# Exact attention scores on TensorE: one 128-row matmul for four heads, or one 25-row matmul for each head in four row groups

## The chip, the cores and the metric

The kernel runs on one core of one Trainium2 chip. The metric is the device time of one execution in microseconds (us); shorter is better. The figures shown are the median of several executions and, for the profile, one execution taken by the hardware profiler.

## The reference

64 sequences of 128 tokens with 128 features go through a gated block. Cut to what matters:

```python
def xattn(x, y):                                   # y: 120 context tokens of 96 features
    q, k, v = split_heads(x @ Wq + bq), split_heads(y @ Wk + bk), split_heads(y @ Wv + bv)   # 16 heads of 8
    scores = einsum('bhqd,bhkd->bhqk', q, k) / sqrt(8)
    return einsum('bhqk,bhkd->bhqd', softmax(scores), v) @ Wo + bo

def ffn(x):
    h = rms(x, n1_w)
    q, k, v = rms(heads(h @ wq.T), qn_w), rms(heads(h @ wk.T), kn_w), heads(h @ wv.T)
    scores = where(causal, einsum('bhqd,bhkd->bhqk', q, k) * 8 ** -0.5, -inf)
    ao = (softmax(scores) @ v) @ wo.T              # first 32 features set to 0
    x = x + ao
    xf = rms(x, n2_w)
    w = top-2 gates of softmax(xf @ gate_w.T)
    return x + w0 * o0(xf) + w1 * o1(xf) + w2 * o2(xf) + w3 * o3(xf)   # first 32 features of the sum set to 0

x = x + tanh(g_xattn) * xattn(layernorm(x), ctx)
x = x + tanh(g_ffn) * ffn(layernorm(x))
```

## The kernel before, in words

The 64 sequences are worked on in 16 groups of four (512 tokens). A group passes through five parts: N (layer norm, projections of the cross-attention), A (cross-attention), B (layer norm, projections of the self-attention), D (self-attention, gates, first expert layers) and M (the other expert layers, output). In one step all five parts run, each on another group, so the kernel is a pipeline: four written-out steps fill it (`RAMP`: `first_group` with N, `second_group` with N and A, `third_group` with N, A and B, `fourth_group` with all but M), a hardware loop runs 12 full steps (t = 3 to 14, order `SCHEDULE`, L160), and four written-out steps empty it (`TAIL`: `last_queries`, `last_self_keys`, `last_self_values`, `last_experts`).

The order of a step is a list written by hand. An entry (part, work, index, ring) is one use of a PSUM bank or a piece of work without one, and every engine walks the same list and does its share of each entry, in the list's order: TensorE fills the bank, ScalarE or VectorE drains it, and two semaphores for each bank, `filled` and `drained`, count the uses. The rings give the banks in turn: `w` has four, `s2` and `f` share the two banks s2a and s2b, `pv` and `t` have one each. `exact(part, b, first)` stands for two uses of the ring `s2`, `estimate` for four score tiles of a sequence, `values` for the four value matmuls of a sequence.

Attention is done in two passes. The *estimate* (work `s1`) computes scores in bfloat16, four row groups of TensorE at a time (L1299; for B with a causal term before it, L1295), and VectorE takes the negative maximum of each row (L1085). The *exact* scores (work `s2`, L1319 to L1336) are computed with float32r operands. For exactness a value is split in a high and a low part, and three products (high x high, low x high, high x low) are summed by stacking them along the contraction: 8 features x 3 = 24 rows a head. A 25th row adds the maximum of the estimate (the query operand holds it, the key operand holds ones).

Before, a chunk c of four heads is one matmul. The key operand `kst` has the four heads' rows interleaved (rows j, j + 4, ... below 96 belong to head j of the chunk, row 96 is ones), and the query operand `qd` has four copies of each column set, one for each head, with zeros in the rows of the other heads:

```python
qd = {p: sb("qd" + p, [P, HT, NT, TOK], F32R) for p in "AB"}
o = bank[0:k, :].rearrange("p (h q) -> p h q", h=HT)
mm(o, kst[p][:, c, b * k:(b + 1) * k], qd[p][:, :, c, b * P:(b + 1) * P],
   start=True, stop=True).then_inc(done, 1)
```

The matmul waits for its own bank only (L1333). ScalarE takes the exponential of the tile of 512 columns into one of eight slots of `probs` (L945). For D, GpSimd then zeroes what the causal mask hides, two tiles at a time (L812). The value matmuls (`pv`, L1337 to L1357) go in four column groups, one for each head j, and wait for the tile (b, c) alone.

The operands travel through DRAM. ScalarE and VectorE write the high and the low part of the projections (L855, L979); SyncE stores them to a scratch tensor (`store_split`, L581 to L590) and loads them back into the stacked rows (`load_stacks`, L592 to L602). The maxima are transposed on TensorE (`mT`, and for the first groups the halves `mH` and `mL`), copied by ScalarE, and brought by a DMA to the 25th row of the query operand: by SyncE (L664, L669), or by ScalarE's own queue for those that `maxima_by_act` (L559) names (L924). The zeros of the query operand are written once at the start, by VectorE (L1016, L1192), GpSimd (L705, L798) and ScalarE (`clear_queries`, L836 to L839). The ones of the key operand are written at L830 and L755.

GpSimd also makes the two causal factors of B's estimate (`causal_factor`, L710): that of the queries in the first step, that of the keys in the third, ahead of squaring B's projections (L823).

Of the kernel before, what the change touches and what calls it, by code (L numbers as in the profile page):

```python
# [31 lines left out]
P = 128  # L32
# [4 lines left out]
HD = 8  # L37
# [138 lines left out]
def second_group():  # L176

    return (one("N", "xT", 0, "pv") + one("N", "k", 0, "t") + one("N", "q", 0, "pv") + one("A", "mL")
            + exact("A", 0, 0) + exact("A", 0, 2) + estimate("A", 0) + exact("A", 1, 0) + exact("A", 1, 2) + values("A", 0)
            + estimate("A", 1) + exact("A", 2, 0) + exact("A", 2, 2) + one("A", "mH", 0, "t") + values("A", 1)  # L180
            + exact("A", 3, 0) + one("A", "oT", 0, "t") + exact("A", 3, 2) + estimate("A", 2) + values("A", 2)
            + one("A", "nT", 0, "t") + one("A", "wo", 0, "t") + values("A", 3) + one("N", "v", 0, "f") + estimate("A", 3)
            + one("A", "oT", 1, "f") + one("A", "nT", 1, "t") + one("A", "wo", 1, "t")
            + one("A", "base", 0, None) + one("A", "stats", 0, None) + one("N", "ctx", 0, None) + one("N", "load", 0, None)
            + one("A", "norm", 0, None))


def third_group():
# [4 lines left out]
            + exact("A", 2, 0) + exact("A", 2, 2) + one("B", "sums", 0, None) + one("N", "stats", 0, None) + one("B", "init", 0, None)  # L193
            + one("B", "root", 0, None) + values("A", 1) + exact("A", 3, 0) + exact("A", 3, 2) + one("B", "scale", 0, None)
            + one("A", "oT", 0, "t") + one("N", "norm", 0, None) + one("B", "qT") + one("B", "kT") + values("A", 2)
            + one("A", "nT", 0, "t") + one("A", "wo", 0, "t") + values("A", 3) + one("B", "v")
            + estimate("B", 0, "ffww") + one("N", "xT", 0, "t") + estimate("B", 1, "wwtp") + one("A", "oT", 1, "f")
            + estimate("B", 2, "fwww") + one("A", "nT", 1, "t") + one("B", "mH", 0, "t") + estimate("B", 3, "ffwp")
            + one("A", "wo", 1, "t") + one("A", "stats", 0, None) + one("N", "q") + one("A", "norm", 0, None)
            + one("N", "k") + one("N", "v"))  # L200


def fourth_group():

    order = of_parts("NABD")
    at = order.index(("D", "s2", (2, 0), "s2"))
    return order[:at] + one("D", "mL", 0, "t") + order[at:]


def last_queries():  # L210
# [4 lines left out]
    at = order.index(("D", "fill", ("e2_l1", 1), "f"))  # L215
# [1235 lines left out]
```

## Time and profile before

| | us |
|---|---|
| median of three executions | 1086.48 |
| lowest and highest | 1086.42 and 1088.23 |
| the profiled execution | 1085.92 |
| its span, first to last instruction | 1084.2 |

The span is the part of the profiled execution that the rows tell of; some 1.7 us lie around it. PE is TensorE's matmuls and PEld its weight loads. A float32 matmul shows as two records in the profile, one for each pass, and so does its load. The end of a matmul in the records is modelled, so the distance from one start to the next says more than the duration.

### The profile page before, as it was taken

The numbers are of one execution on the slowest core, as the hardware profiler recorded it, in microseconds if no ns is written. First come the engines' busy times: TensorE is split into PE (matmuls) and PEld (weight loads), VectorE is DVE, ScalarE is ACT, GpSimd is POOL, SyncE is SP. The second block draws the span as 40 slices with busy tenths as digits, with TensorE's granted clock in tenths as the row PEclk, the third lists the DMA queues.
The fourth block names the chain that finished last, engine by engine and source line by source line (L and its number), as shares of the span: only waits on it lengthen the run. The fifth ranks groups of instructions, "written<-read, shape, count | busy, mean of one in ns | idle before, by whom it ended". The sixth has DMA issues, their size and how long they took to land.

```text
span 1084.2 us, 26207 instructions
## 1 busy us (share of the span) xinstructions
PE 1011.1 (93%) x8649; PEld 628.9 (58%) x8649; DVE 790.0 (73%) x2172; ACT 736.9 (68%) x1334; POOL 338.4 (31%) x463
## 2 busy tenths in 40 slices
PE   7666799999999999999999999999999999999898
PEld 5343456666565566655665665566556565555465
DVE  8546787778778777877777777878777877784633
ACT  6464576677776768777676777767676777757353
POOL 5253315151330505133150514214141422404140
PEclk9779799999999999999999999999999999999999
DMA  6305233334322243333224343332233333221200
GB/s 231 121 27 195 86 101 103 127 115 143 110 94 94 90 126 124 133 114 111 93 73 124 130 127 114 123 99 84 97 129 127 114 134 104 84 67 62 68 1 19
DMA packets 77316, 114.26 MB, mean 105 GB/s; under 512 B 7776, under 2 KB 40160, under 8 KB 77152
## 3 DMA queue, kind: packets, MB, share of 16 engines
q1 hardware_dynamic: 76736, 111.51, 31.7%
q10 hardware_dynamic: 544, 2.28, 0.6%
q8 instruction: 22, 0.36, 0.1%
q14 instruction: 14, 0.11, 0.0%
HBM read 58.97 MB, written 53.74 MB: 104 GB/s over the span
## 4 chain that ended last, share of the span: by engine, by line
PE 64%; DVE 16%; ACT 13%; issue 6%; DMA 1%; ACTq 0%; POOL 0%; DVEq 0%
PE ps_pv L1356 9%; PE ps_w L1382 9%; PE ps_s2a L1335 7%; PE ps_s2b L1335 5%; PE ps_s2a L1394 5%; PE ps_s2b L1401 4%; ACT probs L945 4%; PE ps_t L1218 4%; DVE mpadB L1085 3%; PE ps_w L1401 3%; DVE mpadA L1085 3%; PE ps_w L1267 3%; PE ps_t L1369 3%; PE ps_w L1299 2%; PE ps_w L1218 2%
## 5 line engine op out<-in xcount | busy, mean ns | idle before, releaser
L945 ACT ACTIVATE probs<-ps_s2a 120x512 f32<-120x512 f32 (+1 forms) x256 | 153.6, 600 | 73.7 <-PE ps_s2a L1335 65.3
L1085 DVE TENSOR_REDUCE mpadB<-ps_w 128x4 f32<-128x512 f32 x240 | 148.8, 684 | 24.9 <-PE ps_w L1299 24.9
L1085 DVE TENSOR_REDUCE mpadA<-ps_w 128x4 f32<-128x480 f32 x224 | 131.5, 651 | 41.0 <-PE ps_w L1299 41.0
L945 ACT ACTIVATE probs<-ps_s2b 120x512 f32<-120x512 f32 (+1 forms) x256 | 153.5, 600 | 0.0
L812 POOL TENSOR_SCALAR_AFFINE_SELECT probs<-probs 128x1024 f32<-128x1024 f32 x128 | 140.2, 1095 | 0.0
L1382 PE MATMUL ps_w<-W,hid 128*128 128x96 f32 x1008 | 125.3, 278 | 1.8 <-DVE split_k L979 0.9
L1382 PEld LDWEIGHTS ps_w<-W,hid 128*128 128x128 f32 x1008 | 117.5, 192 | 12.0 <-issue 6.4
L776 POOL TENSOR_TENSOR rB<-vrB,neg_half 128x4 f32<-128x4 f32 x16 | 16.1, 1009 | 204.3 <-DVE veB L972 204.3
L1335 PE MATMUL ps_s2a<-qdA,kstA 128*120 128x512 f32 x128 | 68.5, 535 | 10.6 <-ACT probs L945 9.2
L1114 DVE SCALAR_TENSOR_TENSOR ym<-ps_w,gates,ym 128x96 f32<-128x96 f32 x192 | 47.6, 311 | 39.5 <-PE ps_w L1382 39.5
L1335 PE MATMUL ps_s2a<-qdB,kstB 128*128 128x512 f32 x128 | 65.2, 509 | 11.1 <-DMA qdB<-mTlB 4.5
L1394 PE MATMUL ps_s2a<-hid,W 128*128 128x512 f32 x152 | 74.5, 605 | 0.0
L949 ACT ACTIVATE oT<-ps_pv 128x512 f32<-128x512 f32 x64 | 38.3, 598 | 53.0 <-PE ps_pv L1356 53.0
L941 ACT ACTIVATE hid<-ps_s2a 128x512 f32<-128x512 f32 x75 | 45.0, 600 | 42.6 <-PE ps_s2a L1394 31.0
L1356 PE MATMUL ps_pv<-probs,VA 120*18 120x128 f32 x2048 | 69.3, 276 | 0.0
L1356 PE MATMUL ps_pv<-probs,VB 128*18 128x128 f32 x2048 | 69.3, 276 | 0.0
L952 ACT ACTIVATE onT<-ps_t 128x256 f32<-128x256 f32 x64 | 24.6, 385 | 61.1 <-PE ps_t L1218 61.1
L811 POOL TENSOR_TENSOR tick<-one 128x1 f32<-128x1 f32 x128 | 25.0, 196 | 127.4 <-ACT probs L945 123.6
L1356 PEld LDWEIGHTS ps_pv<-probs,VA 120*18 120x18 f32 x2048 | 50.9, 98 | 22.7 <-issue 21.4
L1356 PEld LDWEIGHTS ps_pv<-probs,VB 128*18 128x18 f32 x2048 | 50.9, 98 | 17.7 <-issue 17.1
L1335 PE MATMUL ps_s2b<-qdA,kstA 128*120 128x512 f32 x128 | 59.0, 461 | 0.0
L1369 PEld LDWEIGHTS ps_t<-W,onT 128*128 128x128 f32 x256 | 39.2, 196 | 32.4 <-issue 20.1
(276 smaller groups left out, 2133.8 us busy)
## 6 DMA issues: line engine op xcount, KB each, us to landing
scratch_Aq<-split_q SPq DMA_DIRECT2D x48, 256.0 KB, 2.4
qdA<-scratch_Aq SPq DMA_DIRECT2D x64, 192.0 KB
scratch_Bq<-split_q SPq DMA_DIRECT2D x48, 256.0 KB, 2.4
scratch_Bk<-split_k SPq DMA_DIRECT2D x48, 256.0 KB, 3.0
qdB<-scratch_Bq SPq DMA_DIRECT2D x64, 192.0 KB
kstB<-scratch_Bk SPq DMA_DIRECT2D x64, 192.0 KB
scratch_Ak<-split_k SPq DMA_DIRECT2D x48, 240.0 KB, 2.4
kstA<-scratch_Ak SPq DMA_DIRECT2D x64, 180.0 KB
```

The lines of the kernel that those rows point to most:

```text
L812: pool.affine_select(out=tile, in_=tile, compare_op=ALU.is_ge, fill=0.0, base=0, pattern=[[0, 2 * HT], [1, P]], channel_multiplier=-1).the ...
L941: nc.scalar.activation(hid[:, HID_AT[index[0]] + index[1], :], bank[:], ACT.Gelu).then_inc(done, 1)
L945: nc.scalar.activation(probs[0:k, slot_of(part, *index), :], bank[0:k, :], ACT.Exp, scale=SCALE if part == "A" else 1.0).then_inc(done, 1)
L1085: nc.vector.tensor_reduce(pair[:, :, c, b % 2] if halves else mneg[p][:, :, c, b], bank[:, 0:HT * k].rearrange("p (h k) -> p h k", h=HT), ...
L1114: ins = nc.vector.scalar_tensor_tensor(out=ym[:, b, KEEP:P], in0=bank[:, b * UP:(b + 1) * UP], scalar=gates[:, b, e:e + 1], in1=y[:, b, KE ...
L1218: ins = nc.tensor.transpose(psum[st.bank[key]][:, b * P:(b + 1) * P], of(b), identf[:])
L1335: mm(o, kst[p][:, c, b * k:(b + 1) * k], qd[p][:, :, c, b * P:(b + 1) * P], start=True, stop=True).then_inc(done, 1)
L1356: ins = mm(psum[st.bank[last]][32 * j:32 * j + VS, at:at + P], VB[p][0:k, first:first + VS], probs[0:k, slot_of(part, b, c), j * P:(j + 1) ...
L1369: ins = mm(bank[:, s * n:(s + 1) * n], onT[:, s * P:(s + 1) * P], w["Wo"] if part == "A" else w["wo"], start=True, stop=True)
L1382: ins = mm(bank[:, b * UP:(b + 1) * UP], hid[:, HID_AT[h] + k, b * P:(b + 1) * P], w[f"down{index[1]}"][:, k * UP:(k + 1) * UP], start=k = ...
L1394: ins = mm(bank[:], w[name][:, k * HID + c * P:k * HID + (c + 1) * P], hid[:, HID_AT[h] + k, :], start=k == 0, stop=k == chunks[-1])
L1401: mm(bank[:], w[name][:, c * P:(c + 1) * P], xfT[:], start=True, stop=True).then_inc(done, 1)
```

## The change

- The query operand shrinks from [128, 4, 4, 512] to [128, 4, 512]: no copies and no zeros. Head j of every chunk lives in rows 32 j to 32 j + 23 of both operands, and row 32 j + 24 holds the maximum (queries) or the one (keys).
- An exact tile is now (b, j): head j of all four chunks, 128 columns for each chunk. It is made of four matmuls with 25 rows, in row group j. Two tiles, j and j + 1, are made together, their matmuls alternating; before the first of the eight, both banks have to be drained. The two tiles' `filled` are counted at their last matmuls.
- The value matmuls read slot j and column block c. As each needs all four tiles of its sequence, they wait for all four (A), or for both masks of the sequence (D).
- The DMA of the maxima goes to four rows. The zeroing is gone, so `clear_queries` and the memsets fall away.
- The low maxima of A's first group are loaded by SyncE (`load_half`), ahead of storing the keys of the second step, no longer by ScalarE.
- GpSimd makes the second causal factor right after the first, in the first step.
- `second_group`, `third_group` and `fourth_group` have new orders; in `last_queries` `mT` stands one entry later; in `last_self_keys` down(2), down(3), estimates and some fills change places and banks. `SCHEDULE`, the loop's order, is the same.

```diff
 def second_group():
-    return (one("N", "xT", 0, "pv") + one("N", "k", 0, "t") + one("N", "q", 0, "pv") + one("A", "mL")
-            + exact("A", 0, 0) + exact("A", 0, 2) + estimate("A", 0) + exact("A", 1, 0) + exact("A", 1, 2) + values("A", 0)
-            + estimate("A", 1) + exact("A", 2, 0) + exact("A", 2, 2) + one("A", "mH", 0, "t") + values("A", 1)
-            + exact("A", 3, 0) + one("A", "oT", 0, "t") + exact("A", 3, 2) + estimate("A", 2) + values("A", 2)
-            + one("A", "nT", 0, "t") + one("A", "wo", 0, "t") + values("A", 3) + one("N", "v", 0, "f") + estimate("A", 3)
-            + one("A", "oT", 1, "f") + one("A", "nT", 1, "t") + one("A", "wo", 1, "t")
+    return (one("N", "xT", 0, "pv") + one("N", "k", 0, "t") + exact("A", 0, 0) + one("A", "mL") + exact("A", 0, 2) + one("N", "q", 0, "pv")
+            + exact("A", 1, 0) + estimate("A", 0) + exact("A", 1, 2) + values("A", 0)
+            + exact("A", 2, 0) + estimate("A", 1) + exact("A", 2, 2) + values("A", 1) + one("A", "mH", 0, "t")
+            + exact("A", 3, 0) + one("A", "oT", 0, "t") + estimate("A", 2) + exact("A", 3, 2) + values("A", 2)
+            + one("A", "nT", 0, "t") + one("A", "wo", 0, "t") + values("A", 3) + one("A", "oT", 1, "f") + estimate("A", 3)
+            + one("N", "v", 0, "f") + one("A", "nT", 1, "t") + one("A", "wo", 1, "t")
...
 def third_group():
-            + exact("A", 2, 0) + exact("A", 2, 2) + one("B", "sums", 0, None) + one("N", "stats", 0, None) + one("B", "init", 0, None)
-            + one("B", "root", 0, None) + values("A", 1) + exact("A", 3, 0) + exact("A", 3, 2) + one("B", "scale", 0, None)
-            + one("A", "oT", 0, "t") + one("N", "norm", 0, None) + one("B", "qT") + one("B", "kT") + values("A", 2)
-            + one("A", "nT", 0, "t") + one("A", "wo", 0, "t") + values("A", 3) + one("B", "v")
-            + estimate("B", 0, "ffww") + one("N", "xT", 0, "t") + estimate("B", 1, "wwtp") + one("A", "oT", 1, "f")
-            + estimate("B", 2, "fwww") + one("A", "nT", 1, "t") + one("B", "mH", 0, "t") + estimate("B", 3, "ffwp")
+            + exact("A", 2, 0) + one("B", "sums", 0, None) + one("B", "root", 0, None) + exact("A", 2, 2)
+            + one("N", "stats", 0, None) + one("B", "init", 0, None) + values("A", 1) + one("B", "scale", 0, None)
+            + one("B", "qT") + one("B", "kT") + one("N", "norm", 0, None) + exact("A", 3, 0) + one("A", "oT", 0, "t")
+            + estimate("B", 0) + exact("A", 3, 2) + values("A", 2) + one("A", "nT", 0, "t") + one("A", "wo", 0, "t")
+            + estimate("B", 1, "ffww") + one("N", "xT", 0, "t") + values("A", 3) + one("A", "oT", 1, "t")
+            + estimate("B", 2, "wwpw") + one("A", "nT", 1, "t") + one("B", "mH", 0, "t") + estimate("B", 3, "ffww")
             + one("A", "wo", 1, "t") + one("A", "stats", 0, None) + one("N", "q") + one("A", "norm", 0, None)
-            + one("N", "k") + one("N", "v"))
+            + one("N", "k") + one("N", "v") + one("B", "v"))
 def fourth_group():
-    order = of_parts("NABD")
-    at = order.index(("D", "s2", (2, 0), "s2"))
-    return order[:at] + one("D", "mL", 0, "t") + order[at:]
+    return (one("D", "mL", 0, "t") + of_parts("NABD", self_attention())
+            + one("D", "wo", 0, "t") + estimate("A", 3) + values("D", 3) + one("D", "oT", 1, "t") + one("A", "mT")
+            + one("B", "scale", 0, None) + one("D", "nT", 1, "t") + one("D", "wo", 1, "t") + one("D", "out", 0, None)
+            + exact("A", 0, 0) + one("B", "qT") + one("B", "kT") + exact("A", 0, 2) + one("N", "stats", 0, None) + one("B", "v")
...
-        qd = {p: sb("qd" + p, [P, HT, NT, TOK], F32R) for p in "AB"}
+        qd = {p: sb("qd" + p, [P, NT, TOK], F32R) for p in "AB"}
...
-        M_ROW = HD * SPLIT * HT
+        HEAD_ROWS, M_ROW = P // HT, HD * SPLIT
...
-            return qd[p][M_ROW:M_ROW + 1, :, :, :].rearrange("p j c (b q) -> p (j c b) q", b=G).bitcast(F32)
+            return qd[p][M_ROW:P:HEAD_ROWS, :, :].rearrange("p c (b q) -> p (c b) q", b=G).bitcast(F32)
...
-                        at = slice(j, M_ROW, HT)
+                        at = rows_of_head(j)
...
-                        for bk, v in st.drains([], key):
-                            pe.wait_ge(drained[bk], v)
-                        o = bank[0:k, :].rearrange("p (h q) -> p h q", h=HT)
-                        mm(o, kst[p][:, c, b * k:(b + 1) * k], qd[p][:, :, c, b * P:(b + 1) * P],
-                           start=True, stop=True).then_inc(done, 1)
+                        if c % 2:
+                            continue
+                        tiles = [(part, "s2", (b, c + half)) for half in range(2)]
+                        for tile in tiles:
+                            for bk, v in st.drains([], tile):
+                                pe.wait_ge(drained[bk], v)
+                        for cc in range(NT):
+                            for half in range(2):
+                                first = (c + half) * HEAD_ROWS
+                                rows = slice(first, first + M_ROW + 1)
+                                ins = mm(psum[st.bank[tiles[half]]][0:k, cc * P:(cc + 1) * P], kst[p][rows, cc, b * k:(b + 1) * k],
+                                         qd[p][rows, cc, b * P:(b + 1) * P], start=True, stop=True)
+                                if cc == NT - 1:
+                                    ins.then_inc(filled[st.bank[tiles[half]]], 1)
...
-                        sources = [(part, "s2", index)] if part == "A" else []
+                        sources = [(part, "s2", (b, j)) for j in range(HT)] if part == "A" else []
...
-                            pe.wait_ge(masked, g * (G * NT // 2) + (b * NT + c) // 2 + 1)
+                            pe.wait_ge(masked, g * (G * NT // 2) + (b + 1) * NT // 2)
...
-                                     probs[0:k, slot_of(part, b, c), j * P:(j + 1) * P], start=i == 0, stop=i == PACK - 1)
+                                     probs[0:k, slot_of(part, b, j), c * P:(c + 1) * P],
+                                     start=i == 0, stop=i == PACK - 1)
```

## Rows read from the trace of the kernel before

**Rows 1.** The page's first part: busy us (share), count of instructions.
```profile
PE 1011.1 (93%) x8649; PEld 628.9 (58%) x8649; DVE 790.0 (73%) x2172; ACT 736.9 (68%) x1334; POOL 338.4 (31%) x463
```

**Rows 2.** Start, steady stage and end: length, busy us of each engine, granted clock (PEclk).
```profile
0.00:160.00 160.00, 117.92 (x996) 73.94 (x996) 106.56 (x276) 90.10 (x157) 58.49 (x95) 0.87 0.38 124
160.00:916.00 756.00, 738.69 (x6457) 459.66 (x6456) 589.99 (x1635) 549.41 (x1003) 233.29 (x302) 1.00 0.35 112
916.00:1084.00 168.00, 154.45 (x1199) 95.26 (x1197) 93.49 (x262) 97.34 (x176) 46.62 (x67) 1.00 0.17 56
```

**Rows 3.** Timeline of TensorE in the steady stage: start us, duration us, what.
```profile
474.49 0.50 PE L1335 MATMUL ps_s2a<-qdB,kstB 128*128 128x512 f32 x1
...
479.74 0.58 PE L1335 MATMUL ps_s2a<-qdB,kstB 128*128 128x512 f32 x1
...
484.16 0.50 PE L1335 MATMUL ps_s2a<-qdB,kstB 128*128 128x512 f32 x1
484.64 0.50 PE L1335 MATMUL ps_s2b<-qdB,kstB 128*128 128x512 f32 x1
485.08 1.07 PE L1356 MATMUL ps_pv<-probs,VB 128*18 128x128 f32 x32
...
507.65 0.47 PE L1335 MATMUL ps_s2a<-qdA,kstA 128*120 128x512 f32 x1
...
514.85 1.07 PE L1356 MATMUL ps_pv<-probs,VA 120*18 120x128 f32 x32
...
518.07 0.48 PE L1335 MATMUL ps_s2a<-qdA,kstA 128*120 128x512 f32 x1
...
518.62 0.60 PE L1218 MATMUL ps_t<-identf,oT 128*128 128x128 f32 x4
...
520.49 1.07 PE L1356 MATMUL ps_pv<-probs,VA 120*18 120x128 f32 x32
...
537.03 0.50 PE L1335 MATMUL ps_s2a<-qdB,kstB 128*128 128x512 f32 x1
```

**Rows 4.** Timeline of ScalarE behind the pair at 484.16.
```profile
484.70 0.60 ACT L945 ACTIVATE probs<-ps_s2a 128x512 f32<-128x512 f32 x1
485.19 0.59 ACT L945 ACTIVATE probs<-ps_s2b 128x512 f32<-128x512 f32 x1
```

**Rows 5.** Timeline of TensorE: runs of matmuls and what follows them.
```profile
505.95 1.92 PE L1382 MATMUL ps_w<-W,hid 128*128 128x96 f32 x16
...
510.10 0.40 PE L1295 MATMUL ps_w<-causal_k,causal_q 32*128 32x512 bf16 x4
510.31 0.40 PE L1299 MATMUL ps_w<-kdB,qTbB 32*128 32x512 bf16 x4
...
511.40 1.07 PE L1356 MATMUL ps_pv<-probs,VA 120*18 120x128 f32 x32
512.40 0.49 PE L1335 MATMUL ps_s2a<-qdA,kstA 128*120 128x512 f32 x1
...
521.49 1.05 PE L1257 MATMUL ps_w<-W,xfT 128*128 128x4 f32 x8
522.40 0.41 PE L1218 MATMUL ps_t<-identf,on 128*128 128x128 f32 x2
```

**Rows 6.** Groups of weight loads: count, busy us, mean ns, idle before.
```profile
L1356 PEld LDWEIGHTS ps_pv<-probs,VA 120*18 120x18 f32 x2048 | 50.9, 98 | 22.7 <-issue 21.4 <-DVE mhalfA L1085 0.4 <-ACT probs L945 0.2
...
L1335 PEld LDWEIGHTS ps_s2a<-qdA,kstA 128*120 128x120 f32 x128 | 23.8, 186 | 44.6 <-ACT probs L945 36.7 <-issue 7.3 <-DMA qdA<-mTlA 0.3
```

**Rows 7.** Timelines of GpSimd, ScalarE's queue and TensorE in the third and fourth step.
```profile
66.28 1.90 POOL L823 TENSOR_TENSOR sq<-qk 128x1024 f32<-128x1024 f32 x1
...
104.96 1.48 ACTq L924 DMA_DIRECT2D qdB<-mTlB  x2
...
109.08 0.79 PE L1335 MATMUL ps_s2a<-qdB,kstB 128*128 128x512 f32 x1 [4.45 <-DMA qdB<-mTlB]
...
125.13 0.69 PE L1218 MATMUL ps_t<-identf,on 128*128 128x128 f32 x2 [3.58 <-DVE on L1126]
```

More of the change, by code:

```diff
@@ L559, in maxima_by_act @@
         def maxima_by_act(st, part, work):
[L561 removed]
+            return (part, work, st.group(part, work)) in (("A", "mH", 0), ("B", "mH", 0), ("D", "mL", 0))
         SETUP_DVE, SETUP_POOL, SETUP_ACT = 1, 1, 1
[L564 removed]
+        A_CLEARED, B_CLEARED = 1, 1
         IDENTITY_MADE, ONE_MADE = 2, 5
@@ L598, in load_stacks, with load_half @@
                     for j in range(HT):
-                        at = slice(j, M_ROW, HT)
+                        at = rows_of_head(j)
                         of = scratch[to + o].rearrange("(c j r) t -> j r c t", j=HT, r=rows)[j]
-                        to_tile = qd[to][at, j, :, :] if o == "q" else kst[to][at, :, :]
+                        to_tile = qd[to][at, :, :] if o == "q" else kst[to][at, :, :]
                         sp.dma_start(to_tile.bitcast(F32), of[:, :, 0:to_tile.shape[-1]]).then_inc(stacks_loaded[to], 16)
+            def load_half(st, part, work):
+                p, half = OP[part], HALVES.index(work)
+                sp.wait_ge(drained[st.bank[part, work, 0]], st.fills(part, work, 0))
+                for b in range(2):
+                    sp.dma_start(half_of_maxima(p, half, b), half_source(p, half, b)).then_inc(half_loaded[p][half], 16)
             def step(st):
@@ L664, in step @@
                         sp.dma_start(maxima_of(OP[part]), mTr[OP[part]][:].bitcast(F32)).then_inc(m_loaded[OP[part]], 16)
-                    elif work in HALVES and not maxima_by_act(st, part, work):
-                        half = HALVES.index(work)
-                        sp.wait_ge(drained[st.bank[part, work, 0]], st.fills(part, work, 0))
-                        for b in range(2):
-                            sp.dma_start(half_of_maxima(OP[part], half, b), half_source(OP[part], half, b)).then_inc(half_loaded[OP[part]][half], 16)
+                    elif work in HALVES and not maxima_by_act(st, part, work) and (st.parts, work) != ("NA", "mL"):
+                        load_half(st, part, work)
             load_x(0)
@@ L834, in _ @@
             nc.scalar.activation(tg[:], vc[:, len(VCOLS) - 2:len(VCOLS)], ACT.Tanh).then_inc(setup_act, 1)
-            def clear_queries(p, first, last, done):
-                nc.scalar.activation(qd[p][:, first:last].rearrange("p j c t -> p (j c t)"),
-                                     one[:].to_broadcast([P, (last - first) * NT * TOK]), ACT.Copy, scale=0.0).then_inc(done, 1)
-            clear_queries("A", 2, 3, setup_act)
             act.wait_ge(setup_dve, SETUP_DVE)
```

37 lines of the change are left out of this document (15 added, 22 removed).

## The prediction

> **What bounds the kernel.** The page's first part says who is busy: TensorE, for 1011.1 of 1084.2 us [rows 1]. Cut by stage, TensorE is busy for 738.69 of the 756 us between 160 and 916 (ScalarE for 549.41), and for 117.92 of the first 160, at a granted clock of 0.87 there and 1.00 later [rows 2]. So there are two places to look at: a steady stage paced by TensorE and its short waits, and a start that waits.
>
> The timeline of TensorE in the steady stage repeats every 62.54 us (474.49 to 537.03) [rows 3]. A step has 16 pairs of exact-score matmuls, two times 512 columns. Their spacing matters, since only two banks take them and ScalarE empties both. Undisturbed, a pair takes 0.55 us (518.07 to 518.62) [rows 3]. Close behind another it waits for the exponentials: the pair at 484.16 takes 0.92 until the value matmuls at 485.08. ScalarE shows why [rows 3, 4]: its exponential starts 0.54 after the first matmul, the next one 0.49 later, each is done after 0.60, and the second bank is free only then. Where one pair directly follows another, ScalarE's round trip is the limit as much as TensorE. 4 pairs of D stand in such a chain (479.74 to the values at 485.08: 5.34 us), 5 of A (507.65 to 514.85: 7.20), and 2 and 2 in short ones (518.07 to 520.49: 2.42). The other 3 stand alone.
>
> **The new matmuls.** A tile of 4 heads was one matmul: 1 weight load and 512 columns. A pair becomes 8 matmuls of 128 columns, alternating over two row groups, with 8 loads of the same 120 or 128 columns: 2048 matmuls and loads in place of 512. Streaming alone would halve if two groups run at once. That groups do run at once is shown: four bfloat16 matmuls of 512 columns in four row groups start 0.21 before the next four [rows 5], and 32 value matmuls in column groups take 1.00, though 8 matmuls with 4 columns each take 0.91 [rows 5]. This last is the price that decides. 4 columns are nothing, so 0.114 each is what a 128-column float32 weight load costs in a row. A load is paid by columns: 186 ns recorded for 120, 98 for 18 [rows 6]. The change cuts rows (128 to 25), not columns, and so keeps each load at its price and has four times as many. I take two groups loading side by side (nearest: the column groups): 4 loads in a row in each group and about one more for entry and last stream, 5 x 0.114 = **0.57 us a pair**, no better than the 0.55 of now. The ends of this unknown: 0.32 if loads hide completely (0.107 for the first, 4 streams at a quarter of the 0.21 row), and 0.97 if the 8 loads go one behind the other (8 x 0.114 + 0.06). A float32 rate of streaming (0.109 a pass, two passes, in two groups) lands at the same 0.98.
>
> That the stream of a group hides behind its next load I read from the 16 matmuls of 96 columns that start at 505.95 and end at the score pair at 507.65 [rows 3, 5]: 0.106 each, the price of the load alone. The Trainium skill (TensorE: Matmul & The Clock Gate, "Part 3: Packing small matmuls") says that a load overlaps with matmuls in flight only when their row groups differ. By that rule load and stream of one group add: 4 x (0.107 + 0.053) + 0.06 = 0.70 a pair, where the row makes 0.57; the time it would give is worked out with the rivals.
>
> **The joint wait.** Both banks must now be empty before the first matmul of a pair, and both are full only at its end. Pair to pair is then at least 0.57 + 0.19 (hop to ScalarE) + 0.49 + 0.60 + 0.05 = 1.90 us, whatever TensorE does between (estimates take 0.3 to 0.5, values 1.00: both under it). Before, the first matmul needed one bank only. Step by step: D chain 3 x 1.90 + 0.57 = 6.27 against 5.34, +0.93. A chain 4 x 1.90 + 0.57 = 8.17 against 7.20, +0.97, and +0.2, as ScalarE also normalises there. Short chains 1.90 + 0.57 = 2.47 against 2.42, +0.05 each. Alone +0.02 each. Sum **+2.2 us a step**. The loop has 12 steps; the other 64 pairs (start and end) are 4 steps' worth: 16 x 2.2 = **+35 us**. Values now need all four tiles of a sequence; they stand behind the next sequence's pairs, which cover that, except where the second half of it is just masked: nothing. Exponentials, masks and their sizes stay.
>
> **Edits elsewhere.** Zeroing of the query operand goes from VectorE, ScalarE and GpSimd in the first 25 us. TensorE waits there for the loaded x and VectorE's maxima, which are the cover; 0, up to -1. Loads of stacks move the same bytes; the maxima go to four partitions instead of one, same bytes; 0. The start's new orders: (a) ScalarE no longer issues the DMA of A's low maxima and the first exponentials come before it; the issue of such a DMA pair takes ScalarE 1.48 [rows 7]: -1. SyncE issues it instead, ahead of storing the keys, which waits for VectorE's low part anyway; A's third sequence is the first to need it. (b) In the second step the transposes of outputs go ahead of the four maxima of an estimate; the same order costs 3.58 in the fourth step, see (e): -2. (c) GpSimd's causal factor leaves the third step, where squares start at 66.28 behind it [rows 7], with 1.90 of their own; root and scale follow, and estimates of B mix with exact scores: -4. (d) D's low maxima go ahead of the fourth step, where TensorE waits 4.45 for their DMA [rows 7]; ScalarE pays the 1.48 for the issue earlier: -3. (e) There too the last estimate goes before scaling; the wait of 3.58 for `on` [rows 7] shortens: -2. Together **-12**, from -20 (each in full) to 0 (the chain of maxima on VectorE takes their place). In the end, where TensorE is busy for 154.45 of 168 [rows 2], `mT`, down(2), down(3) and estimates change places and banks: 0, plus or minus 2.
>
> **Sum.** +35 - 12 = +23. The profiled execution took 1085.92 (span 1084.2), 0.5 under the median of 1086.48; I take the forecast for both: **1110 us**. Its own unknowns: a pair of 0.50 makes a step +1.1 by the same formulas, one of 0.60 +2.7; with the start's -20 and 0 that is 1084 to 1130.
>
> **Rivals.**
> 1. *Packing pays* (faster). If a pair takes 0.32, the spacing is 0.32 + 1.33 = 1.65: D chain 5.27, A chain 7.12, short chains 1.97 (-0.45 each), alone -0.23 each. That is -1.75 a step, -28, and -12: **1046**. For it: groups overlap in rows 5. Against: the price of a load, 0.106 to 0.114 in the same rows. The sign turns at about 0.45 a pair: there +0.75 a step is what the start gives back. The Trainium skill (TensorEngine Tiling (Array Packing), "Theoretical Speedup") promises up to twice for a dimension of 64 or less and up to four times for 32; the scores would come out as in this rival. No row has float32r in row groups.
> 2. *The start pays it back* (no change). At the lower bound of loads side by side, 4 x 0.114 = 0.46 a pair, the spacing is 1.79: +0.49, +0.62, short ones -0.17 each and alone -0.09 each, +0.5 to +0.9 a step, +11, less 12: **1086**.
> 3. *Load and stream of a group add up* (slower). Load 0.107, then 128 columns (a quarter of the 0.21 row, 0.053), four times, and 0.06 for the entry: 0.70 a pair, spacing 2.03: +1.45, +1.8, +0.6, +0.45, so +4.3 a step, +69 - 12: **1143**. The skill's rule named above would give this; the 0.114 a load, with streams hidden, speaks against.
> 4. *Loads one behind the other, or the slow rate* (much slower). 0.97 a pair, spacing 2.30: +2.5, +3.2, +1.7, +1.3 = +8.7 a step: **1213**. For it: no row shows two 128-column float32 loads at once. Against: value matmuls load in four groups at 0.031 each.
>
> **How the numbers follow.** The forecast has 0.42, rival 1 0.28, rival 2 0.07, rival 3 0.10, rival 4 0.13. Faster is rival 1, same is rival 2 (0.2% is 2.2 us, about what can be told from no change here), slower the rest: 0.65. The range takes in rival 1's value, rivals 2 and 3 and the forecast's own span, and leaves out rival 4 and the ends: 1045 to 1155.
>
> **What would show it.** In the loop, the first score matmul of a pair and what follows it stand 0.5 to 0.6 apart; weight loads of the two groups overlap in pairs and follow every 0.11; a pair waits for ScalarE's *second* exponential, starts of neighbouring pairs are 1.9 apart, and the step is 64 to 66 us instead of 62.54. The start: no 4.45 wait on the DMA of the maxima, the steady stage begins about 10 us earlier. I am wrong if a pair takes 0.35 or 0.9, if neighbouring pairs stay 1.2 to 1.6 apart, or if the start gains over 20 or nothing.

## The result and the profile after

The changed kernel takes 1249.38 us (median of four executions, 1241.79 to 1256.94) against 1087.36 for the kernel before on the same chips: a ratio of 1.149 (95% interval 1.142 to 1.156), slower by 162 us. The forecast was 1110 us and the range ended at 1155. The profiled execution took 1250.59 us. Here and below the ratio leaves out executions more than 1.5% above the fastest of their kernel (three of six of `groups`, one of four of `fill2gap` and of `rows64`), while a median in microseconds takes in all.

The page's first part for the changed kernel, against [rows 1], and from its second part the granted clock in 40 slices, in tenths of full speed:

```profile
PE 1137.6 (91%) x10185; PEld 775.3 (62%) x10185; DVE 789.4 (63%) x2170; ACT 735.7 (59%) x1331; POOL 333.4 (27%) x461
...
PEclk9657698879789789989899897977878789868979
```

VectorE and ScalarE do what they did. TensorE has 1536 more matmuls, as the prediction counted, and the line of the clock is new: before, it was at full speed from 132 us on. Start, loop and end of the changed kernel, with the columns of [rows 2] (the eighth figure, behind POOL, is the granted clock):

```profile
0.00:177.00 177.00, 135.63 (x1197) 94.25 (x1198) 104.20 (x281) 85.29 (x156) 54.10 (x93) 0.73 0.42 115
177.00:1047.00 870.00, 819.95 (x7584) 558.10 (x7584) 589.25 (x1621) 549.83 (x997) 232.31 (x300) 0.87 0.36 96
1047.00:1249.00 202.00, 182.04 (x1407) 122.93 (x1405) 95.96 (x271) 100.60 (x180) 47.00 (x68) 0.83 0.19 51
```

The clock has two levels, 1.2 and 2.4 GHz, so a mean of 0.87 over 870 us says that TensorE ran at half clock for 2 x 0.13 x 870 = 226 us of the loop, where it was never at half clock before. The record of the clock behind the mean, stretch by stretch, gives 225 us in the loop, 96 in the start and 69 in the end; before, it gives 41 us, all of it in the start. Times at half clock below are read from this record. The cut is made where a step's transposes of `hb` begin (161.5 and 913.2 in the kernel before). By it, the start is 15 us longer, the loop's twelve steps 118, the end 31.

Two of the twelve steps side by side, one almost at full clock, one not:

```profile
469.83:536.86 67.03, 62.01 (x633) 41.73 (x633) 49.09 (x136) 45.66 (x84) 19.36 (x25) 0.97 0.39 104
815.59:896.06 80.47, 76.62 (x632) 52.33 (x633) 49.28 (x136) 46.03 (x84) 19.36 (x25) 0.77 0.33 87
```

Same work, 13.4 us apart, with 3.4 and 37.5 us at half clock: a microsecond at half clock costs 0.4. A line through all twelve steps says the same: 65.25 us at full clock and 0.387 for each microsecond at half clock. With 62.6 for a step before, the loop's 118 us are 12 x 2.6 = 31 for the step itself and 0.387 x 225 = 87 for the clock.

The new pairs on TensorE's timeline (start, duration), in the chain of A that [rows 3] show from 507.65 to 514.85. Of the eight matmuls of a pair the first pair's stand here in full:

```profile
507.43 0.32 PE L1336 MATMUL ps_s2a<-qdA,kstA 25*120 25x128 f32 x1 [0.58 <-ACT probs L941]
507.44 0.32 PE L1336 MATMUL ps_s2b<-qdA,kstA 25*120 25x128 f32 x1
507.59 0.26 PE L1336 MATMUL ps_s2a<-qdA,kstA 25*120 25x128 f32 x1
507.59 0.26 PE L1336 MATMUL ps_s2b<-qdA,kstA 25*120 25x128 f32 x1
507.69 0.26 PE L1336 MATMUL ps_s2a<-qdA,kstA 25*120 25x128 f32 x1
507.70 0.26 PE L1336 MATMUL ps_s2b<-qdA,kstA 25*120 25x128 f32 x1
507.80 0.26 PE L1336 MATMUL ps_s2a<-qdA,kstA 25*120 25x128 f32 x1
507.80 0.27 PE L1336 MATMUL ps_s2b<-qdA,kstA 25*120 25x128 f32 x1
508.01 0.40 PE L1289 MATMUL ps_w<-causal_k,causal_q 32*128 32x512 bf16 x4
...
509.24 0.31 PE L1336 MATMUL ps_s2a<-qdA,kstA 25*120 25x128 f32 x1 [0.61 <-ACT probs L941]
...
509.80 1.07 PE L1359 MATMUL ps_pv<-probs,VA 120*18 120x128 f32 x32
511.04 0.32 PE L1336 MATMUL ps_s2a<-qdA,kstA 25*120 25x128 f32 x1 [0.17 <-ACT probs L941]
```

The weight loads of the same pair stand in the same rhythm, those of the two groups side by side:

```profile
507.43 0.17 PEld L1336 LDWEIGHTS ps_s2a<-qdA,kstA 25*120 25x120 f32 x1 [0.82 <-ACT probs L941]
507.43 0.17 PEld L1336 LDWEIGHTS ps_s2b<-qdA,kstA 25*120 25x120 f32 x1
507.53 0.18 PEld L1336 LDWEIGHTS ps_s2a<-qdA,kstA 25*120 25x120 f32 x1
507.54 0.18 PEld L1336 LDWEIGHTS ps_s2b<-qdA,kstA 25*120 25x120 f32 x1
```

The two row groups start within 0.01 us of each other, and the pair takes 0.56 to 0.58. Behind the first, a matmul of each group follows every 0.10 with loads of 120 columns, and every 0.11 in D's pairs, whose loads have 128. Starts of neighbouring pairs are 1.81 and 1.80 apart. ScalarE behind the pair at 509.24, against [rows 4]:

```profile
508.59 0.59 ACT L941 ACTIVATE probs<-ps_s2b 120x512 f32<-120x512 f32 x1
509.90 0.60 ACT L941 ACTIVATE probs<-ps_s2a 120x512 f32<-120x512 f32 x1 [0.72 <-PE ps_s2a L1336]
510.39 0.59 ACT L941 ACTIVATE probs<-ps_s2b 120x512 f32<-120x512 f32 x1
```

The pair starts 0.06 behind the end of the second exponential of the one before, and the first exponential 0.66 behind the pair's start: the round trip of the prediction. ScalarE idles for 0.72 here, less where it has other work in between. In the loop TensorE waits 42.5 us for exponentials (total, times, longest), 3.5 a step; the same view of the kernel before shows none:

```profile
PE ps_s2a L1336 <- ACT probs L941: 42.5, 73, 1.0
```

### The profile page after: what moved, and what is told of

It is laid out like the page before. It is cut to its first block, busy times and chain, and to the rows that moved or that the text cites. A ratio compares the mean times of both kernels' runs of the same rounds, so it can differ in the third digit from the quotient of the medians.

```text
span 1248.9 us, 29499 instructions
## 1 busy us (share of the span) xinstructions
PE 1137.6 (91%) x10185; PEld 775.3 (62%) x10185; DVE 789.4 (63%) x2170; ACT 735.7 (59%) x1331; POOL 333.4 (27%) x461
## 4 chain that ended last, share of the span: by engine, by line
PE 71%; ACT 11%; DVE 10%; issue 7%; DMA 1%; SPq 0%; POOL 0%; ACTq 0%; DVEq 0%; POOLq 0%
PE ps_s2a L1336 14%; PE ps_w L1386 12%; PE ps_pv L1359 11%; ACT probs L941 7%; PE ps_s2a L1398 4%; PE ps_t L1212 4%; PE ps_s2b L1405 3%; PE ps_w L1405 3%; PE ps_w L1261 3%; PE ps_w L1212 3%; PE ps_w L1398 2%; DVE mpadA L1080 2%; PE ps_t L1373 2%; PE ps_w L1251 1%; PE ps_s2a L1405 1%
## 5 line engine op out<-in xcount | busy, mean ns | idle before, releaser
L1386 PE MATMUL ps_w<-W,hid 128*128 128x96 f32 x976 | 153.2, 323 | 1.0 <-DVE split_k L975 0.9
L1386 PEld LDWEIGHTS ps_w<-W,hid 128*128 128x128 f32 x976 | 144.3, 235 | 14.6 <-issue 11.9
L1336 PE MATMUL ps_s2a<-qdB,kstB 25*128 25x128 f32 x512 | 103.9, 332 | 37.4 <-ACT probs L941 33.3
L1336 PEld LDWEIGHTS ps_s2a<-qdA,kstA 25*120 25x120 f32 x512 | 81.0, 224 | 90.1 <-ACT probs L941 61.6
L1336 PE MATMUL ps_s2a<-qdA,kstA 25*120 25x128 f32 x512 | 101.0, 326 | 35.2 <-ACT probs L941 30.8
L1336 PEld LDWEIGHTS ps_s2a<-qdB,kstB 25*128 25x128 f32 x512 | 84.3, 231 | 77.2 <-ACT probs L941 48.4
L1336 PE MATMUL ps_s2b<-qdB,kstB 25*128 25x128 f32 x512 | 104.5, 333 | 0.0
L1336 PE MATMUL ps_s2b<-qdA,kstA 25*120 25x128 f32 x512 | 101.3, 327 | 0.0
L1336 PEld LDWEIGHTS ps_s2b<-qdB,kstB 25*128 25x128 f32 x512 | 84.3, 231 | 0.0
L1336 PEld LDWEIGHTS ps_s2b<-qdA,kstA 25*120 25x120 f32 x512 | 80.9, 224 | 0.0
L1359 PEld LDWEIGHTS ps_pv<-probs,VA 120*18 120x18 f32 x2048 | 62.6, 117 | 22.3 <-issue 12.1
```

Source lines behind the costliest of these rows:

```text
L1336: ins = mm(psum[st.bank[tiles[half]]][0:k, cc * P:(cc + 1) * P], kst[p][rows, cc, b * k:(b + 1) * k], qd[p][rows, cc, b * P:(b + 1) * P], ...
L1359: ins = mm(psum[st.bank[last]][32 * j:32 * j + VS, at:at + P], VB[p][0:k, first:first + VS], probs[0:k, slot_of(part, b, j), c * P:(c + 1) ...
L1386: ins = mm(bank[:, b * UP:(b + 1) * UP], hid[:, HID_AT[h] + k, b * P:(b + 1) * P], w[f"down{index[1]}"][:, k * UP:(k + 1) * UP], start=k = ...
```

## The experiments

All are timed against the kernel before on the same chip. Two theories of the clock were to be told apart first: TensorE's idle time at the joint waits, or the small work of the row-group matmuls. For each run the row of its loop is shown, cut at the same place of a step; the first figure behind the stretch is its length, for twelve steps, and the clock is again the eighth.

**The joint wait alone** (`joint`), in the kernel before:

```diff
-                        for bk, v in st.drains([], key):
+                        both = [(part, "s2", (b, c)), (part, "s2", (b, c + 1))] if c % 2 == 0 else []
+                        for bk, v in [w for tile in both for w in st.drains([], tile)]:
                             pe.wait_ge(drained[bk], v)
```

> The kernel before (one 128-row matmul of 512 columns for each tile), with one change: the first matmul of a pair waits until both banks are drained. Theory I (TensorE's idle time at the joint waits makes the clock fall): starts of neighbouring pairs 1.9 apart, idle TensorE of about 3 us a step, granted clock at half for some of the steady stage as in the changed kernel, time 1180 to 1250. Theory II (the clock falls because row-group matmuls with 25 rows, paced by their loads, count as little work, whatever the waits): the same waits, but a clock of 1.00 throughout the steady stage, steps near 65.5 us, time 1125 to 1140.

Measured: 1121.69 us, ratio 1.032 (1.030 to 1.034), +34 us.

```profile
172.00:943.00 771.00, 721.64 (x6435) 450.75 (x6433) 586.17 (x1619) 547.51 (x997) 232.37 (x300) 1.00 0.33 109
```

Steps of 64.25 and a clock of 1.00, with 34.0 us of waits for exponentials between 200 and 900 (34.7 in the changed kernel). Theory I falls for the loop: as much idle time as in the changed kernel does not lower the clock there by itself. In the start it does: 65 us at half clock instead of 41. The joint wait is worth +1.6 of the changed kernel's +2.6 a step. The time lies a little under theory II's 1125 to 1140, as its steps of 65.5 were put too long.

**The tiles of a pair one after the other, each with its own wait** (`apart`), in the changed kernel:

```diff
-                        for cc in range(NT):
-                            for half in range(2):
...
+                        for bk, v in st.drains([], key):
+                            pe.wait_ge(drained[bk], v)
+                        rows = slice(c * HEAD_ROWS, c * HEAD_ROWS + M_ROW + 1)
+                        for cc in range(NT):
+                            ins = mm(bank[0:k, cc * P:(cc + 1) * P], kst[p][rows, cc, b * k:(b + 1) * k],
+                                     qd[p][rows, cc, b * P:(b + 1) * P], start=True, stop=True)
+                        ins.then_inc(done, 1)
```

> The changed kernel, with the two tiles of a pair made one after the other, each waiting for its own bank alone: row groups and 25 rows stay, the joint wait goes, and nothing runs side by side. Loads one behind the other make a pair 0.95 to 1.0 instead of 0.57, so TensorE hardly idles. Theory I (idle time): clock 1.00 in the steady stage, steps 62.5 + 16 x 0.4 minus waits, so 66 to 69, time 1150 to 1180. Theory II (little work counted): the clock falls at least as much as in the changed kernel, time above 1240.

Measured: 1220.77 us, ratio 1.124 (1.121 to 1.127).

```profile
183.00:1025.00 842.00, 825.62 (x7583) 581.97 (x7581) 587.96 (x1618) 548.17 (x996) 232.28 (x300) 0.90 0.37 99
```

The waits for exponentials are down to 7.8 us between 200 and 900, a quarter of those in `joint`, and still 171 us of the loop are at half clock. So theory II holds in kind, though not in size (the clock was to fall at least as far as the 225 us of the changed kernel, and the time to be above 1240): the form of the matmuls lowers the clock with little idle time. The expectation of the pair was wrong in part. Where the second bank was late, a pair took 1.05 (507.20 to 508.25). Where both banks were free, the two tiles ran side by side although they are issued one after the other:

```profile
511.64 0.32 PE L1330 MATMUL ps_s2a<-qdA,kstA 25*120 25x128 f32 x1
511.65 0.32 PE L1330 MATMUL ps_s2b<-qdA,kstA 25*120 25x128 f32 x1
511.80 0.26 PE L1330 MATMUL ps_s2a<-qdA,kstA 25*120 25x128 f32 x1
511.81 0.26 PE L1330 MATMUL ps_s2b<-qdA,kstA 25*120 25x128 f32 x1
```

**The old orders under the changed kernel** (`groups`): the five orders, the causal factor's place and the loading of the low maxima taken back.

> The changed kernel with the first steps, the causal factor, the loading of the low maxima and the last steps' orders as in the kernel before: row groups and joint wait alone. Both theories of the clock: half clock for about as long as in the changed kernel. If the new orders of the start are worth the 12 us of the prediction, this is 10 to 15 us slower than the changed kernel, 1260; if they are worth nothing under the lower clock, the same within 5.

Measured: 1250.2 us (six executions, 1237 to 1263), ratio 1.142 (1.139 to 1.144) against 1.149 (1.142 to 1.156) of the changed kernel: the same within the noise, and not the 10 to 15 us slower that were expected. The profiled execution took 1257.35. Its start is 17 us longer (194 us against 177) with 133 us at half clock instead of 96, its end some 6 shorter and its loop 5, at a clock of 0.88 in both. The gain of the start is smaller than the 25 us between two executions of this one kernel, so this run can't weigh the orders. It does show that row groups and joint wait alone bring 212 us at half clock into the loop.

**The new orders alone** (`orders`), in the kernel before.

> The kernel before with the new orders alone (second, third and fourth step, the moved causal factor, the low maxima by SyncE, the last steps), and the old exact scores. The prediction had 12 us for this: 1075, with the steady stage beginning about 10 us earlier and no wait of 4.45 for the DMA of D's low maxima. Rival: VectorE's chain of maxima takes their place, 1086 within 2.

Measured: 1074.39 us, ratio 0.988 (0.986 to 0.989), -13 us by the medians. The profiled execution took 1075.52, 10.4 under the 1085.92 of the kernel before. Start and loop:

```profile
0.00:154.00 154.00, 116.02 (x1001) 72.18 (x1002) 107.54 (x284) 91.96 (x159) 58.45 (x95) 0.89 0.40 133
154.00:905.50 751.50, 734.45 (x6433) 456.33 (x6431) 585.90 (x1620) 544.49 (x997) 232.36 (x300) 1.00 0.34 111
```

The loop is as before, and the steady stage begins 7.8 us earlier. By the transposes of `hb` in each step, 3.5 of it are won by the third step, 1.5 more by the fourth and 2.8 more by the first full one, and the end is 2.9 shorter. The wait for D's low maxima [rows 7] is gone, but a new one stands in the same step:

```profile
124.90 1.11 PE L1224 MATMUL ps_w<-identf,xn 128*128 128x128 f32 x4 [5.23 <-DVE xn L1007]
```

**Rows and pace, one at a time.** The changed matmuls differ from the old ones in two ways: 25 rows for 128, and a load for every 128 columns instead of every 512. `split4` is the kernel before with four matmuls of 128 columns for a tile, all 128 rows; `rows25` the changed kernel with one matmul of 512 columns:

```diff
# split4
+                        for h in range(HT):
+                            ins = mm(bank[0:k, h * P:(h + 1) * P], kst[p][:, c, b * k:(b + 1) * k],
+                                     qd[p][:, h, c, b * P:(b + 1) * P], start=True, stop=True)
# rows25
+                            mm(psum[st.bank[tiles[half]]][0:k, :].rearrange("p (c q) -> p c q", c=NT), kst[p][rows, 0, b * k:(b + 1) * k],
+                               qd[p][rows, :, b * P:(b + 1) * P], start=True, stop=True).then_inc(filled[st.bank[tiles[half]]], 1)
```

> The kernel before, each exact tile as four matmuls of 128 columns instead of one of 512, all 128 rows, own bank waited for alone: the same products, four times the loads, no row groups. Price: 8 loads of 0.107 in a pair, 0.9 instead of 0.55, so +5 a step at a full clock. If few rows (25 of 128) are what makes the clock fall: clock 1.00, steps 66 to 68, time 1150 to 1175. If it is the pace (a load of 128 columns for each 128 columns streamed): the clock falls as in the changed kernel and the time is above 1200.

> The changed kernel, each tile as one matmul of 25 rows and 512 columns with the key operand of chunk 0 alone (so twelve of the sixteen heads' scores are computed with other heads' keys): row groups, 25 rows and joint wait stay, three of four loads go. Price of a pair 0.107 + 0.213 + 0.06 = 0.38. If few rows make the clock fall: it falls at least as in the changed kernel, time above 1200. If the pace of loads does: clock 1.00 in the steady stage, steps about 64, time 1110 to 1120.

Measured: `split4` 1143.93 us, ratio 1.052 (1.047 to 1.058); `rows25` 1169.47, ratio 1.078 (1.073 to 1.083). Their loops:

```profile
185.00:967.40 782.40, 778.22 (x7585) 567.56 (x7584) 588.12 (x1620) 549.62 (x997) 232.35 (x300) 1.00 0.32 107
```

```profile
167.00:971.30 804.30, 748.47 (x6432) 457.36 (x6432) 588.13 (x1621) 549.26 (x997) 232.47 (x300) 0.93 0.39 104
```

Four times the loads with full rows: clock 1.00 in the loop, steps 65.2 and a time a little under the expected 1150, as part of the loads' price goes into idle time that was there (TensorE idles for 4 us of the loop instead of 17). Few rows with the old number of loads: 116 us at half clock, and a time that neither branch of the expectation had (above 1200, or 1110 to 1120). The rows matter more; with few rows the pace adds to it (225 against 116). `split4` with the joint wait too (`split4joint`) has the pace, idle time and full rows:

> The kernel before, tiles as four matmuls of 128 columns and 128 rows, and the joint wait too: pace and idle time as bad as or worse than in the changed kernel, but full rows. If few rows are a necessary part: clock 1.00 in the steady stage, steps 67.5 to 69, time 1170 to 1185. If pace plus idle time is enough: half clock in the loop, time above 1230.

Measured: 1194.89 us, ratio 1.099 (1.097 to 1.101).

```profile
191.00:998.50 807.50, 782.25 (x7591) 565.77 (x7591) 588.75 (x1622) 551.60 (x997) 232.41 (x300) 1.00 0.32 104
```

Clock 1.00 throughout the loop, steps of 67.25; the 10 us above the expected time lie in start and end (191 and 193 us long, with 96 and 27 us at half clock). But the idle time is not as bad as was meant: TensorE idles for 25 us of the loop, 17.3 of them between 200 and 900 in waits for exponentials, half of the changed kernel's 50 and 34.7. So pace plus half of the idle time is not enough with full rows; the full idle time at this pace is left to the next run.

**More rows at the same pace** (`rows64`): the changed kernel, the two tiles of a pair on rows 0 to 63 and 64 to 127.

```diff
-                                first = (c + half) * HEAD_ROWS
-                                rows = slice(first, first + M_ROW + 1)
+                                rows = slice(half * P // 2, (half + 1) * P // 2)
```

> The changed kernel with taller matmuls at the same pace: the two tiles of a pair use 64 rows each (two heads' rows and their zeroed rest, so every tile holds the sum of two heads' scores) instead of 25; the same eight matmuls of 128 columns, loads, banks and joint wait. If the number of rows counts for the clock: half clock in the loop well below the 225 us of the changed kernel (under 120), time 1150 to 1200, base of a step unchanged near 65.3. If only the pace and the idle time count: about 225 us at half clock, time 1245.

Measured: 1157.24 us, ratio 1.062 (1.059 to 1.064).

```profile
176.00:973.50 797.50, 739.11 (x7588) 496.57 (x7586) 588.39 (x1622) 548.06 (x998) 232.36 (x300) 0.99 0.39 105
```

This is the cleanest comparison. Matmuls, loads, banks and the joint wait are those of the changed kernel, as its timeline shows:

```profile
480.92 0.32 PE L1337 MATMUL ps_s2a<-qdA,kstA 64*120 64x128 f32 x1 [0.17 <-ACT probs L941]
480.92 0.32 PE L1337 MATMUL ps_s2b<-qdA,kstA 64*120 64x128 f32 x1
481.07 0.27 PE L1337 MATMUL ps_s2a<-qdA,kstA 64*120 64x128 f32 x1
...
483.05 0.32 PE L1337 MATMUL ps_s2a<-qdA,kstA 64*120 64x128 f32 x1 [0.95 <-ACT probs L941]
```

TensorE waits for exponentials no less than in the changed kernel (49.4 us in the loop against 42.5), and a step without half clock takes 65.5. The number of rows differs (and what they hold; the query operand is also zeroed once at the start), and the time at half clock in the loop goes from 225 us to 24. The kernel is 92 us faster with more of the array in use. In the start the rows change nothing: 92 us at half clock against 96. The changed kernel was not timed again beside this run on its chip; the kernel before took 1087 us there too.

**Few rows, own wait** (`rows25own`): `rows25` without the joint wait.

> The changed kernel with one matmul of 25 rows and 512 columns for a tile (key operand of chunk 0 for all, so twelve of sixteen heads' scores are computed with other heads' keys), each tile waiting for its own bank. Against the run of that form with the joint wait (1169, 116 us at half clock in the loop, base 64.1) the idle time goes. If idle time and rows add up: less than 60 us at half clock, base 62.5 to 63, time 1100 to 1130. If rows alone decide: about 116 us, time 1140 to 1160.

Measured: 1111.42 us, ratio 1.024 (1.021 to 1.027).

```profile
165.30:928.50 763.20, 739.54 (x6432) 450.34 (x6432) 587.16 (x1621) 547.53 (x997) 232.31 (x300) 0.98 0.41 110
```

31 us at half clock, all in the first five steps of the loop and none in the last seven, against 116 with the joint wait; the base of a step is 62.67, that of the kernel before. So idle time and few rows add up, and few rows alone do not hold the clock down in the steady stage.

**More work for TensorE** (`fill2late`, `fill2gap`). Two float32 matmuls of weight tiles, 128 rows, into the first bank of the pair, overwritten by the scores; in `fill2late` behind the joint wait, in `fill2gap` between its two halves:

```diff
# fill2gap
-                        for tile in tiles:
-                            for bk, v in st.drains([], tile):
-                                pe.wait_ge(drained[bk], v)
+                        for bk, v in st.drains([], tiles[0]):
+                            pe.wait_ge(drained[bk], v)
+                        for _ in range(2):
+                            mm(psum[st.bank[tiles[0]]][:, 0:P], w["Wq"], w["Wo"], start=True, stop=True)
+                        for bk, v in st.drains([], tiles[1]):
+                            pe.wait_ge(drained[bk], v)
```

> The changed kernel with more work: after the joint wait, two float32 matmuls of two weight tiles (128 rows, 128 columns, four records) are made into the first bank before the real ones overwrite it. They cost 4 x 0.107 a pair, some 6 us a step at a full clock. If the clock falls because TensorE does too little work: it comes back to 1.00, steps 71 to 72, time about 1230 to 1245, no slower than the changed kernel in spite of the work. If the clock falls for another reason (the row-group form itself): time above 1320.

> The same two extra matmuls placed in the joint wait: after the first bank is drained, before the second is waited for, where TensorE idles for 0.49 behind the second exponential. They cost little (about 1 to 2 us a step). Too little work: clock 1.00, steps 66.5 to 68, time 1150 to 1175, 80 faster than the changed kernel by doing more. Row-group form itself: clock as in the changed kernel, time 1260 to 1280.

Measured: `fill2late` 1355.57 us, ratio 1.245 (1.240 to 1.250); `fill2gap` 1224.09, ratio 1.125 (1.120 to 1.129). Loops:

```profile
205.50:1148.40 942.90, 886.61 (x8354) 629.20 (x8352) 588.78 (x1620) 550.52 (x997) 232.59 (x300) 0.93 0.33 89
```

```profile
194.00:1041.40 847.40, 825.63 (x8353) 584.63 (x8351) 588.06 (x1620) 549.63 (x997) 232.51 (x300) 1.00 0.37 99
```

Both expectations missed in time: the extra work costs more than I priced (5.4 us a step in the gap, 8.9 behind it, against 1 to 2 and 6). `fill2late` missed in the clock too: it did not come back to 1.00, and the time above 1320 is that of the other branch. Behind the wait, with the idle time left (38.4 us of waits for exponentials between 200 and 900, 34.7 in the changed kernel), 130 us of the loop stay at half clock: extra work of 128 rows helps, but not enough. In `fill2gap` the waits are down to 13.9 us and no part of the loop is at half clock, in an execution of 1236.44 us that was the longest of the four. There the same extra work makes the kernel 25 us *faster*.

**New orders and a busy start** (`orders_busy`): `orders`, and identity matmuls into a bank that is about to be used, in four places of the third and fourth step where TensorE waits.

```diff
+            WHILE_WAITING = {("NAB", "B", "hT"): 14, ("NABD", "B", "hT"): 7, ("NABD", "N", "xT"): 16, ("NAB", "B", "qT"): 8}
...
+                    if (st.parts, part, work) in WHILE_WAITING:
+                        for b, v in st.drains([], key):
+                            pe.wait_ge(drained[b], v)
+                        for _ in range(WHILE_WAITING[st.parts, part, work]):
+                            mm(bank[:, 0:P], identf[:], identf[:], start=True, stop=True)
```

> The kernel before with the new orders, and matmuls of the identity into the waiting bank in four places of the third and fourth step where TensorE waits for VectorE, so that the clock stays up in the start (34 us at half clock in the run with the new orders alone, 1074.4). If the clock follows TensorE's work: half clock in the start under 15 us, time 1066 to 1072. Rival: the extra matmuls end later than the waits they fill, and at half clock take twice as long: 1075 to 1080.

Measured: 1068.39 us, ratio 0.983 (0.981 to 0.984), the fastest of all.

```profile
0.00:148.30 148.30, 123.12 (x1089) 81.10 (x1089) 107.37 (x282) 91.50 (x159) 58.48 (x95) 0.94 0.42 137
```

The start is 5.4 us shorter than in `orders` at a clock of 0.94 instead of 0.89: half clock is down from 34 us to 17, a little above the 15 expected. This version beats both kernels, by 19 and by 181 us.

## Why the prediction was wrong, point by point

- **What bounds the kernel**: right. TensorE and ScalarE's round trip are what the loop follows; VectorE and GpSimd played no part.
- **The price of a pair**, 0.57 from the load price in [rows 5]: measured 0.56 to 0.58. The deciding assumption, that two row groups load side by side, holds (loads and matmuls of the two groups start within 0.01 us of each other), and streams hide behind the next load of their own group. The Trainium skill (TensorE: Matmul & The Clock Gate, "Part 3: Packing small matmuls") has loads overlap only where row groups differ; by that rule a pair was 0.70, and with 0.56 to 0.58 the rows disagree with it. Rivals 1 and 4 fall with this: packing does not pay, and loads do not queue up behind each other.
- **The joint wait**: spacing 1.90 forecast, 1.80 measured, since the exponential starts 0.66 and not 0.76 behind the pair. A step at full clock is 65.25, so +2.6 where +2.2 was worked out; with `joint`, +1.6 of it is the wait by itself. By the prediction's own formulas a spacing of 1.80 makes only +1.4 a step, so that the sum came close is in part luck. In the step that begins at 469.83 the chain of A costs +0.90 (+1.17 forecast), that of D about +0.7 (+0.93) and the short ones nothing, while two stretches with pairs put down as alone (+0.02) cost 0.4 and 0.5; no run shows why. The +34 us of `joint` look like the forecast's +35 for joint wait and new pair together, but only 19 of them are in the loop.
- **The start and the other orders**: -12 forecast, -13 measured by `orders` (-10.4 by the profiled executions). Its split was less good: -7.8 in the start instead of -12, and -2.9 in the end, which was put at 0 within 2; part (d) removed the 4.45 us wait, and a new wait of 5.23 for the normalised x took part of it back. That the zeroing costs nothing was not tested: no run takes it away by itself.
- **The step that failed**: the sum has no term for TensorE's clock. The prediction read 1.00 and 0.87 in [rows 2], said in one clause that the clock was full in the steady stage, and carried every price at full clock into the changed kernel. Without that term the sum was close: 12 x 2.6 + 4 x 2.6 - 11 = +31 on the profiled execution. The profiled executions differ by 164.7 us. The rest, about 134 us, is the clock: 87 in the loop by the line through its steps; in the end, 33.7 us more than in `orders`, of which two steps' worth of +2.6 are 5 and 2 x 0.17 x 202 = 69 us at half clock make 27; the remainder, up to 20, in the start, where half clock rose from 41 us to 96.
- **What lowers the clock**: in the loop, few rows together with idle time or pace. It is shown by `rows64` (same pace and no less waiting, more rows, 225 us to 24) and by `joint`, `split4` and `split4joint` (idle time; pace; pace and half of the idle time, with 128 rows: never in the loop). Neither part of the change does it alone: the 25-row matmuls need the idle time of the joint wait or the pace of their loads beside them (`rows25own` 31 us, `rows25` 116, `apart` 171, changed kernel 225). In the start few rows are not needed for it: it is at half clock for 92 us in `rows64` and for 65, 89 and 96 us in `joint`, `split4` and `split4joint`, against 41 in the kernel before.
- **The rival on the much slower side** had 1213 us at a chance of 0.13, for another reason, and was left out of the range. There was evidence for a clock rival in the rows used: the start, where TensorE does less, was at 0.87.

Zeros in the query operand do not take a row out of use. In the old operand each query column has 25 rows with data (a head's 24 and the maximum) and 103 zeros, as much data as a matmul of the changed kernel has, and the kernels with it keep the full clock in the loop: `joint` with 0 us at half clock against 116 of `rows25`, which has the same joint wait and as few loads, and `split4` with 0 against 171 of `apart`, which has as many loads and little waiting. In `rows64` 50 of the 64 rows hold data.

What stays open: why the steps of one run differ (3 to 37 us at half clock with the same work), whether two matmuls side by side count with the sum of their rows, whether zeros in the key operand (which has none) would count too, and whether the full idle time of the changed kernel at its pace would lower the clock with 128 rows.

## What to carry to other kernels

Where TensorE sets the pace, price its clock as well as its matmuls: a form that uses fewer rows, stretches its work over loads or leaves idle time can cost the rest of the kernel its full clock, here 0.4 us for each microsecond at half clock. Splitting a matmul into row groups costs more if the weight loads, paid by columns, grow with it, and if its PSUM banks have to be waited for together; here it did not pay even without both (`rows25own` 1111 us, `orders` with the old matmuls 1074). In a start that idles at half clock, throw-away matmuls in the waits are cheap: four places gave 6 us here.

## What the runs showed of the hardware that was not expected

- The granted clock depends on how many rows of the array the matmuls use, at the same spacing and with no less idle time: 225 us of the loop at half clock with 25 rows a matmul (changed kernel), 24 with 64 rows (`rows64`). Rows in which the query operand holds zeros count too.
- Work can make a kernel faster: 1024 more matmul records in the idle time of the joint wait brought the clock of the loop from 0.87 to 1.00 and the time from 1249 to 1224 (`fill2gap`).
- Matmuls of two row groups that are issued four and four, one group after the other, start within 0.01 us of each other (`apart`).
- A float32r matmul streams 128 columns behind the next load of its own row group: they follow every 0.10 us with loads of 120 columns and every 0.11 with loads of 128. Two groups side by side take 0.56 to 0.58, where one tile of four matmuls by itself took 0.49 to 0.56 in `apart`.
